# Row sums of the last attention unit on ScalarE, a new order of the attention phase, and one semaphore for each tile of the first input

## What is computed

```python
x = x + attn_a(layernorm(x))      # (2, 1024, 512)
x = x + ffn(layernorm(x))
x = x + attn_b(layernorm(x))
x = x + ffn(layernorm(x))

scores = einsum('bnqd,bnkd->bnqk', q, k) * HEAD_DIM ** -0.5
attn = softmax(where(causal, -inf, scores))
out = einsum('bnqk,bnkd->bnqd', attn, v)          # then @ W_out.T + b_out
ffn(x) = (silu(x @ w_gate.T) * (x @ w_up.T)) @ w_down.T
```

## Time and profile before

| | |
|---|---|
| three runs | 1983.13, 1985.8, 1987.28 us, median 1985.8 |
| profiled execution | 1981.08 us |
| its span | 1979.4 us |
| PE busy | 1954.9 us (99%), 10288 matmul instructions |
| DVE, ACT, POOL busy | 1159.8, 805.8, 982.2 us |
| granted clock, mean | 1.0 |

### The profile page before, as it was taken

The page is one execution under the profiler, slowest core; times in us unless marked ns, Lnnn a source line. Parts: engine busy times, 40 slices in busy tenths (PEclk is TensorE's granted clock), DMA queues, the critical chain, the costliest instruction groups (busy, mean ns, idle before and its releaser), DMA issues.

```text
span 1979.4 us, 27849 instructions
## 1 busy us (share of the span) xinstructions
PE 1954.9 (99%) x10288; PEld 1442.3 (73%) x10288; DVE 1159.8 (59%) x2387; ACT 805.8 (41%) x1478; POOL 982.2 (50%) x767
## 2 busy tenths in 40 slices
PE   7999999999999999999999999999999999999999
PEld 6655588888866568888885656888888565688887
DVE  5777455445677745544567774445457777544544
ACT  2487522221258752222116774322221686432221
POOL 5314469763230436976433053797534215289740
PEclk9999999999999999999999999999999999999999
DMA  5333111121333311311253331121113333012111
GB/s 161 95 88 76 34 43 54 54 64 43 85 87 76 76 44 32 107 53 54 75 139 87 76 76 44 36 62 53 53 43 86 87 80 82 24 43 64 54 43 43
DMA packets 58821, 132.37 MB, mean 67 GB/s; under 512 B 10560, under 2 KB 11584, under 8 KB 58688
## 3 DMA queue, kind: packets, MB, share of 16 engines
q1 hardware_dynamic: 58688, 130.60, 24.2%
HBM read 75.51 MB, written 4.19 MB: 40 GB/s over the span
## 4 chain that ended last, share of the span: by engine, by line
PE 94%; ACT 2%; DVE 2%; DMA 1%; SPq 1%; issue 1%; POOL 0%; ACTq 0%; DVEq 0%; POOLq 0%
PE bank L1354 11%; PE bank L1356 11%; PE bank L1355 11%; PE bank L1488 11%; PE ring L1354 11%; PE ring L1355 11%; PE ring L1356 11%; PE bank L1461 8%; PE ring L1430 7%; PE ring L1345 1%; ACT prob L861 1%; SPq L555 1%; DMA area<-kq_parts 1%; ACT kq_parts L844 0%; ACT area L940 0%
## 5 line engine op out<-in xcount | busy, mean ns | idle before, releaser
L861 ACT ACTIVATE prob<-bank 128x512 f32<-128x512 f32 (+1 forms) x512 | 273.1, 570 | 158.5 <-PE bank L1461 133.0
L655 POOL TENSOR_SCALAR area<-w_stage 128x1024 fp32r<-128x1024 f32 x126 | 144.3, 1146 | 374.2 <-PE bank L1356 190.0
L657 POOL TENSOR_TENSOR area<-w_stage,area 128x1024 fp32r<-128x1024 f32 x126 | 302.0, 2397 | 10.5
L1168 DVE TENSOR_TENSOR x<-x,bank 128x512 f32<-128x512 f32 x256 | 170.4, 684 | 232.2 <-PE bank L1356 231.6
L732 POOL TENSOR_SCALAR_AFFINE_SELECT prob<-prob 128x512 f32<-128x512 f32 x128 | 82.7, 647 | 446.5 <-ACT prob L861 356.1
L1098 DVE CUSTOM_DVE_ANT_0 xn<-ring,mask_row 128x384 bf16<-128x384 f32 (+7 forms) x384 | 244.2, 663 | 66.8 <-PE ring L1430 65.3
L1354 PE MATMUL ring<-xt_hi,area 128*128 128x512 f32 x672 | 263.7, 392 | 1.3 <-DVE area L1201 1.3
L1355 PE MATMUL ring<-xt_lo,area 128*128 128x512 f32 x672 | 262.0, 390 | 0.0
L1356 PE MATMUL ring<-xt_hi,area 128*128 128x512 f32 x672 | 261.8, 390 | 0.0
L1461 PE MATMUL bank<-area 98*128 98x512 f32 (+3 forms) x768 | 244.7, 374 | 2.6 <-ACT prob L861 1.4
L1461 PEld LDWEIGHTS bank<-area 98*128 98x128 f32 x768 | 133.1, 188 | 125.1 <-ACT prob L861 83.6
(11 more groups left out here) (172 smaller groups left out, 3612.5 us busy)
## 6 DMA issues: line engine op xcount, KB each, us to landing
w_stage<-ffn_w SPq DMA_DIRECT2D x96, 512.0 KB, 3.5
area<-kq_parts SPq DMA_DIRECT2D x336, 128.0 KB, 2.4
w_stage<-attn_w SPq DMA_DIRECT2D x32, 512.0 KB, 4.3
area<-attn SPq DMA_DIRECT2D x48, 128.0 KB, 4.0
x<-x_in SPq DMA_DIRECT2D x16, 256.0 KB, 3.9
out<-x SPq DMA_DIRECT2D x16, 256.0 KB, 2.0
bias_rows<-row_bias SPq DMA_DIRECT2D x8, 256.0 KB, 3.9
masked<-x_in SPq DMA_DIRECT2D x4, 256.0 KB, 4.2
```

The source lines that it names most:

```text
L655: pool.tensor_scalar(hi, src, 1.0, 0.0, ALU.mult, ALU.add).then_inc(w_hi_done, 1)
L657: pool.tensor_tensor(lo, src, hi.bitcast(F32), ALU.subtract).then_inc(w_split, 1)
L861: act.activation(prob[:, step % PROB_BUFS, h, off:], scores_at(u, j, h), ACT.Exp, scale=SCALE).then_inc(prob_ready, 1)
L1168: dve.tensor_tensor(x[:, t, :], x[:, t, :], row_bank(s, n)[:, :], ALU.add).then_inc(rows_drained, 1)
```

## The change

`SUMMED` becomes (3, 5, 7). So unit 7, the last one of a pass, gets no sum groups on PE, no copy of denominators on ACT and no reciprocals on DVE; it gets 16 row sums, the logarithms and the shift. All five order tables are written anew, for all units. The input's eight tiles get a semaphore each. Ahead of the first pass DVE takes the statistics tile by tile and the variances pair by pair, and takes over the low parts of the first two weight slots from POOL; POOL takes the inverse deviations pair by pair and fills the rows of ones only after the split of the third weight slot. `deviations` only counts the extra one.

```diff
--- before.py
+++ after.py
@@ -156,7 +156,7 @@
 PROB_BUFS = 3
-SUMMED = (3, 5)
+SUMMED = (3, 5, 7)
@@ -200,43 +200,43 @@
 ORDER = (
...
-    "ssffvsffsfsfsvffssffvsfsfvsfsfssfssfsvsffssvsfsfsvsssffssssvss",
-    "sfsfsvsfsvsfsfsvvfssssfssssv",
-    "ssvvvssfssvssvssvssffssvssvssfssfssvvvvvssfssssfssssvvvv",
+    "svffsfsfsvsfsffsfsvfsffsfsfsvsffssfsvfssvfssvfssfssfsfsssfvfssfss",
+    "svfsvfssssvsffsssvvvvssfsfsssv",
+    "ssvssfssvssssvssfssfssfssfssvvssvssfssssfssssvvv",
 )
...
@@ -327,7 +327,7 @@
-        x_loaded = [sem(f"x_loaded{c}") for c in range(CHUNKS)]
+        x_loaded = [sem(f"x_loaded{t}") for t in range(TT)]
@@ -462,6 +462,10 @@
+        def deviations(it, ln, c):
+
+            return it * 2 * CHUNKS + ln * CHUNKS + c + 2
@@ -562,7 +566,7 @@
             def load_x(batch, c):
                 for t in range(c * CT, (c + 1) * CT):
-                    sp.dma_start(x[:, t, :], x_in[batch, t * P:(t + 1) * P, :]).then_inc(x_loaded[c], 16)
+                    sp.dma_start(x[:, t, :], x_in[batch, t * P:(t + 1) * P, :]).then_inc(x_loaded[t], 16)
@@ -764,16 +768,17 @@
             pool.wait_ge(const_ready, CONSTS)
+            for r in range(2):
+                pool.wait_ge(var_ready, r + 1)
+                t = slice(2 * r, 2 * r + 2)
+                pool.tensor_tensor(rstd[:, t], var_eps[:, t], minus_half[:, 0:2], ALU.pow).then_inc(rstd_ready, 1)
+            pool.wait_ge(rstd_ready, 2)
+            pool.wait_ge(w_split, len(V_SLOTS))
+            for i in range(len(V_SLOTS), AHEAD):
+                split_weights(0, i)
+            pool.wait_ge(w_split, AHEAD)
             pool.memset(k_stack[3 * HEAD:3 * HEAD + 2, 1:, :, :].bitcast(F32), 1.0).then_inc(ones_ready, 1)
             pool.wait_ge(ones_ready, 1)
-            inverse_deviation(0, 0, 0)
-            pool.wait_ge(xn_ready, CT)
-            for i in V_SLOTS:
-                hi, lo = w_part(i, slice(0, SLOT))
-                pool.wait_ge(w_hi_done, i + 1)
-                pool.tensor_tensor(lo, w_stage[:, i, :], hi.bitcast(F32), ALU.subtract).then_inc(w_split, 1)
-            for i in range(len(V_SLOTS), AHEAD):
-                split_weights(0, i)
@@ -1015,17 +1020,34 @@
+            def first_normalise(r):
+
+                dve.wait_ge(rstd_ready, r + 1)
+                for t in (2 * r, 2 * r + 1):
+                    dve.tensor_scalar(xn_tile(t), x[:, t, :], mean_var[:, t, 0:1], rstd[:, t:t + 1],
+                                      ALU.subtract, ALU.mult).then_inc(xn_ready, 1)
+
+            def first_weights_lo(i):
+
+                hi, lo = w_part(i, slice(0, SLOT))
+                dve.wait_ge(w_hi_done, i + 1)
+                dve.tensor_tensor(lo, w_stage[:, i, :], hi.bitcast(F32), ALU.subtract).then_inc(w_split, 1)
+
             def late_stats(it, t):
 
-                if t == CT and it == 0:
-                    dve.wait_ge(x_loaded[1], 16 * CT)
+                if it == 0:
+                    dve.wait_ge(x_loaded[t], 16)
@@ -1321,10 +1341,16 @@
-            chunk_stats(0, 0)
-            normalise_pair(0, 0, 0)
-            normalise_pair(0, 0, 1)
+            for t in range(CT):
+                dve.wait_ge(x_loaded[t], 16)
+                tile_stats(t, x[:, t, :])
+                if t % 2:
+                    variances(t + 1, range(t - 1, t + 1))
+            first_normalise(0)
+            first_weights_lo(0)
+            first_normalise(1)
             xt_to_lo(0, 0, 0)
+            first_weights_lo(1)
             xt_to_lo(0, 0, 1)
```

More of the change, by code:

```diff
@@ L215 @@
     "xxxxxxx",
[L216 to L223 removed]
+    "exeeeeeeeeeee",
+    "eeeeoxeexeeeeeeeereereereerreerereeeererr",
+    "ereoeexrxeeererrerexee",
+    "exeeeeeeoeeeerererererereeeereerexerxeerererr",
+    "eereerereeoxeeexee",
+    "eeeeeeeeoeeeereeerereereereereererererer",
+    "eereerereeoerreeee",
+    "eeoeeeeeeeeeeeeeeeeeeeeeeeeeexox",
 )
 DVE_ORDER = (
[L228 to L230 removed]
+    "nmnnmnnnnmmmmmmmqmmmmqmmmqmmqmmmqmmqmmmmmqmmmmmqmmmmmmmmmmmmmmmmmqmrmmqrrmmrmrmmmmmrmmrmmmmmrmmmrrrrrmrr"
+    "mmmmmhmmmrmmqmmmmmqmmmmmmmmmmmmrmmmmrrrmrmmmmmmmmrrmrhmmmqmmmmqmmmmmmmmmmmmmmmmmmrrmrmrmmrrmmmrrmmhmrrrr"
+    "rrrrmmmmnnnmml",
 )
 POOL_ORDER = (
[L235 removed]
+    "bbdwbbmmmmwmbmbmmmmmmwwmwmmmmmwmaammbammmamammamwabmdmmmwd",
 )
 SP_ORDER = (
[L239 removed]
+    "klkkklkklkkmkkkmkkkkmkkklkkmkklkmkkklkkmlkkkkmmll",
 )
@@ L740, in add_out_bias @@
                     if first_layer(it):
-                        pool.wait_ge(x_loaded[t // CT], (it // LAYERS + 1) * (16 * CT))
+                        for n in range(t, t + CT):
+                            pool.wait_ge(x_loaded[n], (it // LAYERS + 1) * 16)
                     pool.wait_ge(xn_ready, it * 2 * TT + t + CT)
@@ L1017, in chunk_variance, with variances @@
                 n = it * 2 * TT + ln * TT + (c + 1) * CT
-                dve.wait_ge(stats_done, 2 * n - CT)
-                for t in range(c * CT, (c + 1) * CT):
+                variances(n, range(c * CT, (c + 1) * CT))
+            def variances(n, tiles):
+                dve.wait_ge(stats_done, 2 * n - len(tiles))
+                for t in tiles:
                     dve.bn_aggr(mean_var[:, t, :], stats[:, t, :]).then_inc(stats_done, 1)
                 dve.wait_ge(stats_done, 2 * n)
-                t = slice(c * CT, (c + 1) * CT)
+                t = slice(tiles[0], tiles[-1] + 1)
                 dve.tensor_scalar(var_eps[:, t], mean_var[:, t, 1], EPS, None, ALU.add).then_inc(var_ready, 1)
+            def first_normalise(r):
[7 more added lines that the diff above has]
+                dve.tensor_tensor(lo, w_stage[:, i, :], hi.bitcast(F32), ALU.subtract).then_inc(w_split, 1)
             def late_stats(it, t):
-                if t == CT and it == 0:
-                    dve.wait_ge(x_loaded[1], 16 * CT)
+                if it == 0:
+                    dve.wait_ge(x_loaded[t], 16)
                 elif t == CT and first_layer(it):
```

38 lines of the change are left out of this document (11 added, 27 removed).

## The result

The changed kernel took 2004.6 us (median of 5 runs, 1999.23 to 2008.23) beside 1986.7 for the kernel before (5 runs, 1983.13 to 1988.04): ratio 1.0093, 95% interval 1.0080 to 1.0105. The forecast was 1981.8, with a range of 1965 to 1990: the change made the kernel slower, and the time lies outside the range. The profiled execution took 2004.6 us, its span is 2002.9, 23.5 over that of before; the mean granted clock is 0.99.

The account below looks back on a forecast made before the run. TensorE was taken as the bound (94% of the chain). Per pass 5.96 - 4.5 - 0.1 - 0.7 - 0.1 + 0.3 = 0.9 us, four passes 3.5, start 0.5: 1981.1 becomes 1977.1, by the median 1981.8; range 1965 to 1990.

Parts of the forecast that it names:

- The chain over ScalarE: Units 5 to 7: row sums and exponentials in order on ACT delay unit 7's transposed maxima, costing 4.5 us a pass.
- PE's own 32.9: Time from unit 5's first transposed score to unit 7's maxima that PE would need by itself: 30.05 plus 2.85 us.
- lower bound of 1.1: Least wait in us a pass at unit 7's maxima, if ACT's work were spread so row sums end by 33.
- The removed sums: Unit 7's products with ones leave PE: 5.96 us saved per pass, 23.8 us in four passes.
- Work taken from PE counts in full wherever nothing else is late: Whole kernel: PE fills 94% of the chain that ended last, so the removed sums were counted at their full 5.96 us a pass.
- that wait: Transposes for the second normalisation lose a run of sums ahead of them: 0.1 us a pass, an estimate.
- Waits behind the maxima: After unit 7's maxima: 0.1 us before its first score, 0.7 at the output projection, 0.1 at the second normalisation, per pass.
- Units 0 to 5: New order of the other units: between +0.8 and -0.8 us per pass, taken as a gain of 0.3.
- rival B: ACT idles 2.1 us before unit 7's maxima, which come later than 38.3; 1.2 us more a pass, 1990 us; chance 0.19.
- The start: Start of the run: earlier first transposes, but POOL's order holds the second pair; gain 0.5 us, bounds 0 and 3.
- POOL's chain: At the start: weight split, both memsets, two bias additions, then the second chunk's inverse deviation, done at 28.8 us.
- everything else counts only through waits of PE: Whole kernel: work on engines other than PE was priced only by the length of the PE waits it causes.

Follow-up runs that it names:

- 16 more activations: Kernel before, order and row sums unchanged, with 16 extra ScalarE activations a pass in units 5 and 6, at the changed kernel's row-sum places: 2017.1 us, ratio 1.0169.
- short row sums: Changed kernel with unit 7's 16 row sums taken over 128 columns instead of 640 to 1024: 1993.7 us, ratio 1.0049 to the kernel before.
- the pauses: Kernel before with two, then five, extra ScalarE activations of 640 columns in one piece in unit 6 of each pass: 1993.0 us and 2010.1 us.
- filler: Changed kernel with the first matmul of 14 of unit 7's score tiles issued twice, 3.2 us more TensorE work a pass: 2002.6 us, 1.0101 to the kernel before.
- start-only kernel: Changed kernel's code with the five order tables and row-sum units of the kernel before: 1984.3 us, ratio 1.0007 to the kernel before.

## Why the prediction was wrong

**The chain over ScalarE was the right mechanism.** Forecast was a wait of 4.5 us a pass at unit 7's maxima; in the last pass, where the clock stayed up, the maxima came at 38.1 instead of 37.4, so the wait was 5.2 against PE's own 32.9: 0.7 too low, inside the bounds. ACT's sequence had no gap and the forecast length (26.8 us for 26.6); it began 0.7 late. The run with 16 more activations, with nothing else changed, shows that the load does it. But the lower bound of 1.1 was wrong: with short row sums 3.4 of the 5.2 remain, so PE's own 32.9 is not what the stretch falls to when ACT has room.

**The removed sums.** 5.96 us a pass fits the changed order: 6.1 were saved behind the maxima, where 1.9 us of work went ahead of them (7.1 - 5.2) and 1.8 of waits came in. As a value of its own it was not right: without a new order it can't be told from 0 in the total. "Work taken from PE counts in full wherever nothing else is late" hid the question, since the way from the output projection to the second normalisation was late at once. I priced that wait at 0.1; it is 1.9 in the old order, and is not there in the new one, where the projection has moved.

**The tail and the other units.** Waits behind the maxima: 0.9 forecast, 1.8 worked out (5.96 + 1.9 - 6.1), of which the trace records only 0.6 as idle time of PE, and not where I had put most of it (op:0 did not wait). Units 0 to 5: 0.3 of gain forecast, none seen. With the 0.7 of the chain these make 1.9 us a pass: 0.9 gained became 1.0 lost. That is close to rival B's price of 1.2, which I gave 0.19, but not by B's mechanism: ACT did not idle on the way, and with the clock up the maxima stayed under B's mark of 38.3.

**The start.** 0.5 us of gain forecast, 2.9 of loss measured at the first maxima, 2.0 with before's order. POOL's chain was right to within 0.8 us (28.8 forecast, 29.6 measured), and the low parts took 1.23 and 1.21 us, not 1.4. But PE had come to the transposes 4.1 us earlier, waited, and then ran at half clock; I had compared start times only.

**The term that was missing** is the clock. The step that failed is "everything else counts only through waits of PE": a wait also costs what comes behind it, and the sum had nothing for that. The profiled execution was forecast at 1977.1 and took 2004.6, 27.5 more: 7.6 for the four passes at full clock (1.9 each), 3.4 for the start, and 16.5 that only some passes lose, of which 13 stand in stretches with the clock down. Those stretches hold longer waits too, so 13 is the most that the clock can have cost in them.

The runs of the changed kernel nearly order themselves by their mean clock: 0.993 with 1999.2 us, 0.992 with 2001.5, 0.991 with 2005.1, 0.990 with 2004.6, 0.987 with 2008.2. Of before, 26 runs at 1.000 have a median of 1981.1, 6 at 0.997 one of 1986.4. That is 1.5 to 1.8 us for each 0.001; carried on to 1.000 the changed kernel would take 1987 to 1990, an estimate, and so lose 6 to 9 us. The segments gave 7 in another way. That the clock falls behind waits is shown by the pauses; what decides in which pass it does stays open, and that the changed kernel would run at such a time with its clock held up was not shown: the one attempt with filler failed.

## What to carry to other kernels

When PE is the bound by a hair, price a new wait with the clock behind it: here a recorded wait of 1.3 us cost 1.6 us in two passes and 3.2 in two others. Before counting matmuls as saved, take them out alone and see who is late next; sometimes they are the cover of a chain. And before an engine with "10 us to spare" is given more, put that load on it in the old order: one run answers it.

## What the runs showed of the hardware

- One and the same recorded wait of 1.3 us was followed by a granted clock of 1.00 in two passes and by 0.66 over 5 us in two others of one execution. The Trainium skill (TensorE: Matmul & The Clock Gate, HAM oscillation — how this bites in real kernels) tells of matmuls at half clock behind each wait for a transfer; the trace agrees that it is paid again and again, and adds that waits for exponentials do it too, and that it does not happen each time.
- In the first pass of the start-only kernel a single wait of 1.37 us for a stacking transfer is followed by 8 us at 0.61 and 7 at 0.71; the segment from unit 4's to unit 5's maxima took 36.7 us instead of 32.8. In the kernel before the wait at this place was 0.7 us, and the clock stayed at 1.00.
- A DVE subtraction of 128x1024 with both inputs in SBUF took 1.23 and 1.21 us while POOL stood idle; while POOL is busy the like one takes 2.40 in the mean.
